# First value products ahead of the first chunk's segment sum on TensorE, in place of two unread products there

## The reference

```
xn = _layernorm(x)
s  = xn + mamba2(layernorm(xn));  s = s + mlp(layernorm(s))
h  = xn + attention(rms(xn));     h = h + moe(rms(h))
x  = x + s * silu(h)
# the scan of mamba2, for each token:
h = h * dA[:, :, None, None] + (dt_t[:, :, None] * x_t)[..., None] * B_t[:, None, None, :]
y = jnp.einsum('bhpn,bn->bhp', h, C_t)
# attention:
scores = jnp.einsum('bhqd,bhkd->bhqk', q, k) * HD ** (-0.5)
attn = softmax(where(causal, scores, -inf));  ao = einsum('bhqk,bhkd->bhqd', attn, v)
```

## Time and profile before

| what | value |
|---|---|
| median of 3 runs | 847.98 us (847.05 to 848.3) |
| the profiled execution: its time | 848.16 us |
| its span in the profile | 846.4 us |
| outside the span | 1.76 us |
| TensorE matmul busy | 777.2 us, 92% |
| VectorE busy | 613.7 us, 73% |
| ScalarE busy | 510.2 us, 60% |
| GpSimd busy | 293.8 us, 35% |

### The profile page before, as it was taken

How to read it: one execution, slowest core, us unless ns; L and a number is a source line. 1 busy time by engine, 2 the same in 40 slices (tenths; PEclk the granted TensorE clock), 3 DMA queues, 4 the chain that set the end, 5 groups by cost and what they waited for, 6 DMA issues and landing times.

```text
span 846.4 us, 18186 instructions
## 1 busy us (share of the span) xinstructions
PE 777.2 (92%) x5482; PEld 486.3 (57%) x5482; DVE 613.7 (73%) x1491; ACT 510.2 (60%) x968; POOL 293.8 (35%) x577
## 2 busy tenths in 40 slices
PE   2779999999999999999899999999999999999997
PEld 1555564756547565665647565475556656475646
DVE  2685569785887868787697868878587877978624
ACT  2426784577753775467845677537754678456662
POOL 5413534143512616036240445216160262404400
PEclk9998999999999999999999999999999999999999
DMA  4000000000000000000000000000000000000000
GB/s 169 2 8 15 14 1 2 9 16 26 0 2 13 28 3 0 8 13 26 0 0 8 14 25 0 2 7 27 11 0 8 13 27 0 0 8 14 26 0 13
DMA packets 15145, 11.73 MB, mean 14 GB/s; under 512 B 1040, under 2 KB 13968, under 8 KB 14992
## 3 DMA queue, kind: packets, MB, share of 16 engines
q1 hardware_dynamic: 15120, 11.43, 4.5%
HBM read 7.76 MB, written 2.10 MB: 12 GB/s over the span
## 4 chain that ended last, share of the span: by engine, by line
PE 54%; DVE 18%; issue 12%; ACT 10%; POOL 4%; DVEq 1%; POOLq 0%; ACTq 0%
PE R L455 33%; PE S L455 13%; DVE sb_mx L1242 9%; ACT sb_pr L1136 3%; PE S L460 3%; DVE sb_cv L1260 2%; POOL sb_pr L1784 2%; PE R L573 2%; POOL sb_lnv L1680 2%; PE R L460 1%; DVE sb_x L1478 1%; ACT sb_junk L1053 1%; DVE sb_rqk L1387 1%; ACT sb_sq L1034 1%; PE R L616 1%
## 5 line engine op out<-in xcount | busy, mean ns | idle before, releaser
L1136 ACT ACTIVATE sb_pr<-S 128x768 f32<-128x768 f32 (+1 forms) x192 | 161.9, 886 | 111.8 <-PE S L455 111.8
L1242 DVE TENSOR_REDUCE sb_mx<-S 128x2 f32<-128x256 f32 (+3 forms) x256 | 198.0, 818 | 32.9 <-PE S L455 31.9
L1784 POOL TENSOR_SCALAR_AFFINE_SELECT sb_pr<-sb_pr 128x256 f32<-128x256 f32 (+1 forms) x192 | 98.7, 519 | 145.3 <-ACT sb_pr L1136 144.0
L455 PE MATMUL R<-sb_pr,sb_va 128*32 128x512 f32 (+3 forms) x1024 | 88.8, 441 | 3.4 <-POOL sb_pr L1784 1.2
L455 PE MATMUL R<-sb_W,sb_pr 128*128 128x96 f32 (+1 forms) x512 | 69.5, 276 | 0.0
L455 PE MATMUL R<-sb_xfT,sb_W 128*128 128x512 f32 x144 | 69.2, 602 | 0.0
L1771 POOL TENSOR_TENSOR sb_seg_r<-sb_seg_v,sb_seg_head 128x512 fp32r<-128x512 f32 x8 | 8.3, 1040 | 174.7 <-ACT sb_seg_v L1167 174.7
L455 PE MATMUL S<-sb_kT,sb_qT 32*128 32x256 f32 (+3 forms) x512 | 56.7, 385 | 13.0 <-DVE sb_mx L1242 10.2
L455 PEld LDWEIGHTS R<-sb_W,sb_pr 128*128 128x128 f32 x512 | 63.5, 192 | 3.8 <-issue 3.5
L455 PEld LDWEIGHTS S<-sb_kT,sb_qT 32*128 32x128 f32 x512 | 27.6, 183 | 65.5 <-DVE sb_mx L1242 58.2
L455 PE MATMUL S<-sb_qT,sb_kT 32*128 32x256 f32 (+3 forms) x512 | 56.5, 385 | 7.6 <-ACT sb_pr L1136 7.6
(11 more groups left out here) (230 smaller groups left out, 1726.1 us busy)
## 6 DMA issues: line engine op xcount, KB each, us to landing
sb_xin<-x SPq DMA_DIRECT2D x9, 256.0 KB, 2.8
sb_W<-weights SPq DMA_DIRECT2D x1, 2290.0 KB, 10.4
sb_qT<-sb_mT SPq DMA_DIRECT2D x128, 4.0 KB
sb_xres<-x SPq DMA_DIRECT2D x8, 256.0 KB, 2.8
out<-sb_xres SPq DMA_DIRECT2D x7, 256.0 KB, 2.3
sb_cT<-sb_xact SPq DMA_DIRECT2D x8, 128.0 KB, 2.3
sb_W<-weights SPq DMA_DIRECT2D x1, 514.0 KB, 4.6
sb_cst<-consts SPq DMA_DIRECT2D x1, 328.0 KB, 3.2
```

The costliest lines, as they stand in the source:

```text
L455: return pe.matmul(o, lhsT, rhs, start=start, stop=stop, skip_group_check=True)
L1136: act.activation(pr[:, e % 4, :, 0:n], S[pair_of_exp(e)][:, :, 0:n], ACT.Exp).then_inc(p_sb, 1)
L1242: o = dve.tensor_reduce(mx[:, n // P - 1, g, heads[0]:heads[1] + 1], found[:, :, at_col:at_col + n], AX.X, ALU.max, negate=True)
L1784: pool.affine_select(out=keep, in_=keep, compare_op=ALU.is_ge, fill=0.0, base=0, pattern=pattern, channel_multiplier=-1)\
```

## The change

In the pass through `stage_a`, the two unread products that stood in `segments(r, 0)` ahead of the segment sum are gone, and with them their waits. The value products of the first two pieces (`weigh_values(r, 0)`) stood behind the scores of piece 3 and the maxima scores of step 3; they now stand behind those of piece 2, ahead of `segments(r, 0)`. Nothing else is changed.

```
             def segments(r, c):
 
-                if c == 0:
-                    pe.wait_ge(moe_sb, at(moe_sb, r, 4 * E))
-                    pe.wait_ge(segl_sb, at(segl_sb, r, 1 + T))
-                    dense(R[1][:, 0:256], 2)
                 pe.wait_ge(segl_sb, at(segl_sb, r, 1 + T))
                 pe.wait_ge(segr_sb, at(segr_sb, r, 1))
...
                     if e == 2:
+                        weigh_values(r, 0)
                         segments(r, 0)
...
                         segments(r, g)
-                    if g == 0 and u == 3:
-                        weigh_values(r, 0)
```

More of the change, by code:

```diff
@@ L590, in segments @@
             def segments(r, c):
[L592 to L595, removed]
                 pe.wait_ge(segl_sb, at(segl_sb, r, 1 + T))
```

## The result

The changed kernel takes 857.83 us (median of 6 runs, 852.93 to 860.59) against 847.93 before (6 runs, 847.05 to 850.01). The ratio is 1.0111, with a 95% interval of 1.0085 to 1.0138: it is slower by 9.9 us. I had forecast 847.8 in a range of 846.0 to 849.3, and a slower kernel with a chance of 0.13. The profiled execution took 860.59 us with a span of 858.9.

What follows compares the result with a forecast made beforehand. Two strands, TensorE's queue and VectorE's, were taken to bind together. Seven rounds gain 1.26 us, the first pass loses 0.39: −0.87, or +0.48 with one more half-clock stretch; the middle is 847.8 us, range 846.0 to 849.3.

Steps and rivals of the forecast that it cites:

- The place of the segment sum: In stage_a's full rounds, value products fill the wait; the sum starts 0.18 us earlier, 1.21 us behind the masking of step 2.
- The freed place: Behind step 3's masking, 0.99 us leaves TensorE's queue; two idle times of some 0.4 us appear around piece 4's scores.
- The gain of a round at full clock: Each of seven full rounds becomes 0.18 us shorter, 98.37 us in place of 98.55.
- both strands: TensorE's queue and the path over es, wm and VectorE's maxima, both ending at step 4's maxima scores within 0.06 us.
- The first pass: At half clock there, value products take 1.85 us against 1.46 for the unread ones; 0.39 us lost.
- The clock: Half-clock stretches, 1.35 us each, seen in the finishing part: two as before or one more, weighed alike.
- Rival 3: More half-clock stretches, in stage_a's new gaps or the finishing part, 1.35 us each; 849.8 us with two more; chance 13%.
- Its extreme: Two more stretches plus one in each of seven rounds, +8.6 us, 856.6 us.
- a shorter round changes the number of stretches in the finishing part: Rounds 0.18 us shorter fall differently in time, so the finishing part's two stretches in seven rounds need not stay two.

Runs made afterwards that it cites:

- drop_only: The kernel before without the two unread products, the value products left in their old place; 852.86 us, ratio 1.0057.
- changed_again: The changed kernel timed and profiled a second time, with no edit; 858.10 us, ratio 1.0118 to before.
- both_ahead: The changed kernel with the two unread products put back ahead of the segment sum, behind the value products; 873.38 us, ratio 1.0286 to before.
- thin_filler: The changed kernel with seven unread products of 4 columns ahead of the scores of piece 4; 867.32 us, ratio 1.0222 to before.
- fill_two: The changed kernel with two unread products of 256 columns ahead of the scores of piece 4; 848.12 us, ratio 0.9994 to before.
- longer: The kernel before with one more unread product per full round, in the experts' output products; 849.19 us, ratio 1.0008.
- fill_gate: The kernel before with one unread product in each of two short waits of the finishing part; 846.88 us, ratio 0.9982.

## Why the prediction was wrong, point by point

- **The place of the segment sum: right.** 1.21 us behind the masking of step 2, as forecast, and no idle time ended by `sb_x`. The maxima scores of step 4 did wait for VectorE, 2.86 us behind the segment sum where I had 2.94; the scores of piece 4 came 0.70 us earlier against the masking of step 2 (3.18 in place of 3.88 us), where I had 0.6.
- **The freed place turns into waiting: right in kind.** The gaps are 0.22, 0.22 and 0.45 us where I had two of 0.4. The first of them, ahead of the maxima scores of step 3, I had left out: these hang on VectorE's maxima of step 2, which I noted, but I did not count the time ahead of them as a gap.
- **The gain of a round at full clock: mis-sized.** 0.27 us in place of 0.18. The difference is on VectorE's strand: the segment sum took 0.50 us in place of 0.58, and `es` started 0.62 us behind it in place of 0.69. I also took both strands to end within 0.06 us; drop_only shows that TensorE's own was 0.32 us shorter. That did no harm here, since VectorE's strand stayed the later one.
- **The first pass: right in size, short in kind.** Where the half clock lasted (changed_again), the value products took 1.86 us for 1.85 forecast, and the sum came 2.19 us behind the masking of step 2 in place of 1.65, 0.54 lost for 0.39 forecast. In the first profile the half clock ended during the value products, and 0.32 was lost. What followed in both, a second stretch, I had not counted; it cost 2.33 in the first profile.
- **The clock: this is the step that failed.** I wrote of the rule on short idle times between groups of matmuls that "by the rows above they needn't", counted the new gaps at nothing in the sum, and priced every stretch at 1.35 us. The rows that I had could not say so: they showed the place with its value products behind the segment sum, and not without them. Nor did a gap of 0.32 us ahead of the segment sum say anything of two or three behind it. In the runs, with the value products gone from behind the segment sum or the wide filler gone ahead of it, falls came in three of seven full rounds (changed, drop_only) or in all (both_ahead), and where the stretch is twice as long it costs 2.96 us and not 1.35. I also read the two stretches of before from the starts of their windows; by the clock in the earlier trace rows they began at 317.9 and 614.8 and lasted 3.4 us each. The rule of the Trainium skill, "TensorE: Matmul & The Clock Gate", section "A second HAM failure mode: psum-queue depth-cycling", stood against the change, and both_ahead agrees with it: it has all the matmul work of before, 1.32 us of waiting in two pieces, and 25 us more. thin_filler does not fit it: there the clock fell at a place where TensorE had no idle time.
- **Rival 3 was the case**, with its place named, its price per stretch under half of what it was, and a chance of 0.13. Its extreme, 856.6 us, is close to the median of 857.83 by luck: it counts one stretch of 1.35 us in each of seven rounds, and the profile has four of about 2.2 to 2.7 us and, ahead of the changed place, 3.35 us that are not the change's.
- **That a shorter round changes the number of stretches in the finishing part: borne out, in one profile each.** fill_two had three, before two, longer none. In fill_two they took back what the shorter rounds gained; in the changed kernel's first profile there were two, as before.

Left open: how much of the 9.9 us is the value products' move and how much the unread products' removal. drop_only costs 4.3 us, both_ahead 25, and the two edits together 9.9, so that they don't add up. The sum of the gaps does not order them either (1.17, 1.32 and 0.89 us in drop_only, both_ahead and changed). The place of each in time and what work stands beside it may count too, and no run here took these apart. Open as well is why six of twelve profiles, the changed kernel's first among them, had a stretch at half clock from about 29 us, in code that all of them share. In the changed kernel's first profile most of the 3.35 us ahead of the changed place come from it, of the 12.4 by which the two profiled spans differ; how often the timed runs had it is not known. It is not what makes the changed kernel slower: with such a stretch in their profiles longer and fill_gate still had 0.992 and 0.988, and no execution of changed had more than 0.982.

## What to carry to other kernels

A product that nothing reads, or a real one beside waits, may be what keeps TensorE at full clock; before one is moved or taken out, look for stretches at half clock in windows of half a microsecond, in every round and in more than one execution, since neither the busy shares nor the chain showed them here. A transfer of work out of a place with waits needs, as its bad case, a fall of the clock there in every round (both_ahead: seven of up to 3 us, and 25 us in all), and the cheapest test is the one that moves this work and nothing else. When a saving per round does not arrive, compare rounds with and without a stretch: the saving may be there and the clock may take it back. Here a short filler of wide products in the right wait brought it out.

## What the runs showed of the hardware

- A busy TensorE did not by itself keep its clock: with 1.60 us of products of 4 columns in the place of the value products the falls stayed (867.32 us), with one product of 256 columns, in 0.59 us, there were none in `stage_a` of the full rounds (848.58 us).
- The stretches at half clock came in lengths of about 3.4, 6.8, 10.2, 17 and 20.5 us in the profiles. Those of 3.4 us cost 1.35 us a round, of 6.8 some 3 (changed, both_ahead), of 10.2 some 4.0 (thin_filler).
- A shorter round at full clock was not a shorter round on the mean: with rounds of 98.34 (fill_two) and of 98.55 us (before) the mean over the falls was 99.00 and 98.99 us, and rounds of 98.83 (longer) had no fall and beat both. That the length of the round is what decides it is not shown.
- Scores for the exponentials and for the maxima, each on 32 rows of the array, overlapped when both could start: 0.13 us between their starts in drop_only, in place of 0.45.
